# Cross attention normalised through the rows that shift its scores, with a new order on every engine

## The chip, the cores and the metric

The kernel runs on one core of a Trainium2 chip. A core has a matrix engine (TensorE, PE, whose weight loads the profile lists apart as PEld), a vector engine (VectorE, DVE), a scalar engine (ScalarE, ACT), a general engine (GpSimd, POOL) and DMA queues, which SyncE (SP), ACT and POOL feed. Each engine works through its own instructions strictly in order and waits on semaphores. The metric is the device time of one execution in microseconds.

## What is computed

Eight batches of 512 tokens by 512 features pass through two layers, each behind a layer norm and each added to its input.

```python
# cross attention: 16 heads of 32, 77 context tokens, masked by length
q, k, v = heads(ln(x) @ Wq), heads(ctx @ Wk), heads(ctx @ Wv)
A = softmax(where(mask, q @ k.T / sqrt(32), -1e20))       # 512 x 77 per head
x = x + (A @ v) @ Wo
# self attention: q, k, v and o are each a main matrix plus two low-rank experts,
# which a small gate picks for the whole batch element
h = ln(x); top, gates = top2(relu(mean(h) @ gw1.T) @ gw2.T)
x = x + o(softmax(q(h) @ k(h).T * SCALE) @ v(h))          # 512 x 512 per head
```

## The kernel before

All matrix work is on PE, batch after batch. In each layer 16 heads are four jobs of four heads. Cross attention of batch b, job i, goes like this. `q1` projects the normalised x; its result is split in a high and a low part and copied by ACT (`q1_rows`) and DMAs into a stack of rows, so that one product over 96 rows is exact enough. `csc` computes, for each of the four token tiles t, the scores of the four heads side by side in one PSUM bank (128 tokens by 4 x 78), and DVE takes the negated row maxima from it (L1040). `cross_shift` turns the 16 columns of maxima into 16 rows on PE (L1280), DVE splits these in high and low part (L1055, L1057), and ACT issues two small DMAs (`move_shift`, L900) that put the two parts into the stack as two further rows. `csT` (L1295) then computes the scores transposed, keys by tokens, and the two extra rows subtract each token's maximum in the same product. ACT takes exp (L914) into `probs1`. `cpv` (L1311) multiplies these with V, and `cden` (L1319) multiplies the same probabilities with ones, which gives the row sums, spread over the head's 32 rows. ACT copies the product of `cpv` out (`cacc`, L930, into the tile that the profile calls xhat), DVE takes the reciprocal of the sums in four pieces (`cinv`, L1075), POOL multiplies (`cdivide`, L754), and `out1` (L1217 with Wo) projects. Four jobs are summed in `out1`, so its last quarter needs job 3. Then come DVE's `residual1`, the second layer norm, the transposes (`xpose`, L1211), the gate, the effective weights (`weff`), and self attention with the same pattern: `sc` (L1274, row maxima at L1048), `shift`, `sT` (L1302, exp at L925), `pv` (L1331), sums over keys on POOL (`psum`, L780 and L784), `den` (L1340), `inv` (L1075), `divide` (L754), `out2` (L1217).

Scores of both layers share a ring of two PSUM banks, transposed scores another of two, and three banks (`pj`) go to whatever step needs one. The cross attention of batch b+1 is interleaved with the self attention of batch b, so the pattern repeats with every batch. Only batch 0's cross attention has no self attention beside it. There PE also runs the products of the context (`context_keys`, L1190; `context_values`, L1202) and dummy products (`warm`, L1182).

What sets the order is a table: `CALENDAR` gives a time to each step of a batch, `OWN` gives exceptions, and every engine walks through all steps in the order of these times and issues its part of each (`Engine.walk`). The times are no clock: they only sort. Semaphore waits are computed from the same order.

## Time and profile before

| | |
|---|---|
| three runs | 1421.96, 1423.52, 1429.27 us (median 1423.52) |
| span of the profiled execution | 1426.7 us, from the first to the last instruction |
| PE busy | 1391.0 us, 97% |
| DVE, ACT, POOL busy | 951.9 us (67%), 861.3 us (60%), 679.8 us (48%) |
| mean granted TensorE clock | 0.980 of full |
| PE's share of the chain that ended last | 85% |

No time is given for the profiled execution apart from its span, and the span is 3.2 us above the median of the runs. A busy share is an average. The chain that ended last is followed back from the last instruction: each piece of it is what the next one had to wait for. A clock of 1.00 in a stretch is 2.4 GHz, and 0.50 is 1.2 GHz.

### The profile page before, as it was taken

How to read it: one execution, taken by the hardware profiler on the slowest of the kernel's cores; microseconds unless marked ns; L12 is line 12 of the kernel's file. 1: busy time of each engine (PE TensorE's matmuls, PEld its weight loads, DVE VectorE, ACT ScalarE, POOL GpSimd, SP SyncE). 2: the span in 40 equal slices, each digit the busy share in tenths (PEclk: the TensorE clock that was granted, in tenths of full speed). 3: DMA queues.
4: the chain of work that ended last, by engine and by line, in shares of the span. 5: the costliest groups of instructions: out<-in, count | busy, mean ns of one | idle time of the engine just before them, and what ended most of it. 6: DMA issues, size and time to landing. Idle time of an engine off the chain costs nothing.

```text
span 1426.7 us, 17122 instructions
## 1 busy us (share of the span) xinstructions
PE 1391.0 (97%) x5704; PEld 702.4 (49%) x5704; DVE 951.9 (67%) x1687; ACT 861.3 (60%) x1499; POOL 679.8 (48%) x411
## 2 busy tenths in 40 slices
PE   8998999999999999999999999999999999999987
PEld 5545444545455444555555445455545454444432
DVE  4454577766767677767777677767777677666572
ACT  2425474866577663975658664876648665565652
POOL 2011143545555362556445463555625455465675
PEclk9889999999999999999999999999999999999999
DMA  7514233522434224522234224332235323233210
GB/s 252 143 53 133 46 68 96 153 76 46 98 110 108 75 54 125 137 61 76 68 111 123 75 59 135 110 85 67 58 104 152 76 46 97 64 101 79 81 39 30
DMA packets 78767, 130.81 MB, mean 92 GB/s; under 512 B 26374, under 2 KB 32134, under 8 KB 75607
## 3 DMA queue, kind: packets, MB, share of 16 engines
q1 hardware_dynamic: 74007, 128.55, 33.4%
q10 hardware_dynamic: 4672, 1.17, 0.4%
q8 instruction: 45, 0.74, 0.2%
q14 instruction: 43, 0.35, 0.1%
HBM read 66.08 MB, written 12.21 MB: 55 GB/s over the span
## 4 chain that ended last, share of the span: by engine, by line
PE 85%; ACT 7%; issue 2%; DMA 2%; POOL 2%; DVE 1%; ACTq 0%; SPq 0%; POOLq 0%
PE pj L1217 43%; PE scT L1302 9%; PE sc L1274 8%; PE acc L1331 7%; PE sc L1263 4%; PE pj L1247 2%; PE pj L1311 2%; PE scT L1295 2%; PE pj L1319 2%; PE pj L1340 2%; DMA qs<-shift 2%; PE pj L1190 1%; ACT xhat L810 1%; PE pj L1202 1%; PE pj L1211 1%
## 5 line engine op out<-in xcount | busy, mean ns | idle before, releaser
L925 ACT ACTIVATE probs<-scT 128x512 f32<-128x512 f32 x512 | 288.9, 594 | 303.9 <-PE scT L1302 300.8
L1048 DVE TENSOR_REDUCE negmax<-sc 128x1 f32<-128x512 f32 x512 | 338.0, 684 | 140.7 <-PE sc L1274 139.7
L784 POOL TENSOR_TENSOR probs_sum<-probs_sum,probs 128x1024 f32<-128x1024 f32 x128 | 300.2, 2365 | 57.4 <-ACT probs L925 57.3
L1075 DVE RECIPROCAL inv_sum<-pj 128x128 f32<-128x128 f32 x256 | 225.0, 921 | 59.9 <-PE pj L1340 39.2
L1274 PE MATMUL sc<-ks,qs 96*128 96x512 f32 x512 | 260.1, 541 | 2.4 <-DVE negmax L1048 1.6
L1217 PE MATMUL pj<-XT,Wqk 128*128 128x512 f32 x512 | 257.3, 598 | 0.6 <-DVE Wqk L1140 0.6
L1302 PE MATMUL scT<-qs,ks 99*128 99x512 f32 x512 | 250.9, 517 | 6.2 <-DMA qs<-shift 3.2
L780 POOL TENSOR_TENSOR probs_sum<-probs 128x1024 f32<-128x1024 f32 x64 | 151.4, 2372 | 173.8 <-ACT probs L925 173.8
L790 POOL TENSOR_TENSOR uv_stack<-UVS_sb,uv_stack 96x1024 fp32r<-96x1024 f32 x32 | 75.7, 2367 | 178.1 <-ACT UVS_sb L832 178.1
L1302 PEld LDWEIGHTS scT<-qs,ks 99*128 99x128 f32 x512 | 94.7, 191 | 124.5 <-ACT probs L925 60.4
L754 POOL TENSOR_TENSOR xhat<-xhat,inv_sum 128x128 f32<-128x128 f32 (+1 forms) x56 | 45.1, 806 | 207.7 <-DVE inv_sum L1075 207.7
L1274 PEld LDWEIGHTS sc<-ks,qs 96*128 96x128 f32 x512 | 97.9, 192 | 92.0 <-issue 47.1
L1331 PE MATMUL acc<-probs,V 128*32 128x512 f32 x1024 | 137.2, 613 | 0.0
L1217 PE MATMUL pj<-Wvo,ctx2T 128*128 128x512 f32 x256 | 131.0, 602 | 0.7 <-POOL ctx2T L754 0.7
L1217 PE MATMUL pj<-XT,Wq_sb 128*128 128x512 f32 x256 | 127.2, 601 | 1.1 <-ACT XT L844 1.1
L914 ACT ACTIVATE probs<-scT 77x512 f32<-77x512 f32 x128 | 72.4, 588 | 91.2 <-PE scT L1295 91.0
L1217 PE MATMUL pj<-Wvo,XT 128*128 128x512 f32 x256 | 122.4, 600 | 0.0
L1217 PEld LDWEIGHTS pj<-XT,Wqk 128*128 128x128 f32 x512 | 95.2, 191 | 54.7 <-issue 35.4
L1217 PE MATMUL pj<-Wo_sb,xhat 128*128 128x512 f32 x256 | 115.8, 599 | 0.0
L1263 PEld LDWEIGHTS sc<-keys,qsc 97*128 97x128 f32 x480 | 66.1, 196 | 34.5 <-issue 23.5
L893 ACT ACTIVATE ks<-stage_hi 32x512 fp32r<-32x512 f32 x128 | 80.1, 626 | 3.3 <-ACT stage_hi L868 0.6
L893 ACT ACTIVATE qs<-stage_hi 32x512 fp32r<-32x512 f32 x128 | 80.2, 626 | 2.7
(103 smaller groups left out, 1716.6 us busy)
## 6 DMA issues: line engine op xcount, KB each, us to landing
Wqk<-in_WmT SPq DMA_DIRECT2D x16, 1024.0 KB, 6.1
Wvo<-in_WmT SPq DMA_DIRECT2D x16, 1024.0 KB, 6.5
UVS_sb<-in_UVS SPq DMA_DIRECT2D x64, 192.8 KB, 3.4
qs<-stage_lo SPq DMA_DIRECT2D x136, 64.0 KB, 2.2
qs<-qs SPq DMA_DIRECT2D x34, 256.0 KB, 3.0
X<-in_x SPq DMA_DIRECT2D x8, 1024.0 KB, 6.0
ks<-stage_lo SPq DMA_DIRECT2D x128, 64.0 KB, 2.0
ks<-ks SPq DMA_DIRECT2D x32, 256.0 KB, 3.0
```

The costliest lines, as they stand in the source:

```text
L780: nc.gpsimd.tensor_tensor(probs_sum[:, pair], probs[:, 0, pair], probs[:, 1, pair], ALU.add)\
L784: nc.gpsimd.tensor_tensor(probs_sum[:, pair], probs_sum[:, pair], probs[:, kt % 2, pair], ALU.add)\
L790: nc.gpsimd.tensor_tensor(uv_stack[:].rearrange("p s n -> p (s n)"), UVS_sb[:, n, 0:2 * D], uv_stack[:].rearrange("p s n -> p (s n)").bitc ...
L893: nc.scalar.activation(stack[0:DH, slot, jj, :], stage_hi[jj * DH:(jj + 1) * DH, n, :].bitcast(F32), ACT.Copy).then_inc(sems["rows_copied" ...
L925: nc.scalar.activation(probs[:, kt % 2, jj, :], scT[:, ST[step], :], ACT.Exp, scale=SCALE)\
L1048: nc.vector.tensor_reduce(negmax[:, 0, n:n + 1], sc[:, SC[step], :], AX.X, ALU.max, negate=True)\
L1075: nc.vector.reciprocal(inv_sum[:, INV[use], at], pj[:, PJ[left_in(full)], at])\
L1217: mm = nc.tensor.matmul(pj[:, p, :], lhsT, rhs, start=(dc == 0), stop=(dc == DC - 1))
L1263: mm = nc.tensor.matmul(sc[:, SC[step], j * NKP:(j + 1) * NKP], cross_stack(b, i)[0:MASK_ROW + 1, j, t * P:(t + 1) * P], keys1[0:MASK_ROW ...
L1274: nc.tensor.matmul(sc[:, SC[step], :], qs[0:3 * DH, slot, jj, t * P:(t + 1) * P], ks[0:3 * DH, slot, jj, :], start=True, stop=True).then_i ...
L1302: nc.tensor.matmul(scT[:, ST[step], :], ks[0:ROWS, slot, jj, kt * P:(kt + 1) * P], qs[0:ROWS, slot, jj, :], start=True, stop=True).then_in ...
L1331: mm = nc.tensor.matmul(acc[jj * DH:(jj + 1) * DH, 0, :], V2[:, kt, v_slot(b, j), jj * DH:(jj + 1) * DH], probs[:, kt % 2, jj, :], start=( ...
```

## The change

Row sums are no longer found on PE from the finished probabilities, but on DVE and ACT from the untransposed scores, before the transposed product. For each tile t of `csc`, DVE adds the negated maximum to the scores (`cless`, 128 x 312, from PSUM to SBUF), ACT takes exp in place (`cexp`), and DVE sums each head's 77 columns (`csum`). For each job ACT takes the logarithm of the 16 sums per token (`cln`), and DVE scales it by -1/SCALE beside the maxima. `cross_shift` turns 32 columns instead of 16, ACT issues four small DMAs instead of two, and the stack gets two more rows. `csT` subtracts maximum and logarithm together, and exp gives probabilities that are divided already. `cden`, `cinv` and `cdivide` are gone; `out1` waits only for `cacc`. `csc`'s bank is released by `cless` instead of by the row maxima. The buffer of reciprocals shrinks to one, so `inv` of a job waits for `divide` of the job before. A table set that holds both exp and log is named at ACT's start. The layer norm of the next batch waits for `gate_top` of this batch.

```diff
-    "cden": (-963, -556, -444, -35),
+    "cln": (-1339, -1033.2, -557.9, -171),
...
+CROSS_ROWS = SHIFT_ROW + 4
+INVERSES = 1
+LESS_SLOTS = 2
...
     if kind == "cross_shift_move":
-        return {"cross_shift_moved": 32}
+        return {"cross_shift_moved": 64}
...
-INV, INV_BEFORE = ring([step for step in STEPS if step[0] in ("divide", "cdivide") and step[3] == pieces(step[2]) - 1], 2)
+INV, INV_BEFORE = ring([step for step in STEPS if step[0] == "divide" and step[3] == pieces(step[2]) - 1], INVERSES)
+LESS, LESS_BEFORE = ring([step for step in STEPS if step[0] == "cless"], LESS_SLOTS)
...
+            nc.scalar.preload_act_table_set("natural_log_exp_and_others")
...
             def normalize(step, b, half):
-                before = ("out1", b, TT - 1, DC - 1) if half else ("xpose", b - 1, 1, TT - 1)
+                before = ("out1", b, TT - 1, DC - 1) if half else ("gate_top", b - 1)
...
             def cross_shift_move(step, b, i):
-                move_shift(1, cross_stack(b, i), "cross_shift_moved", b, ("cross_shift", b, i))
+                dst = cross_stack(b, i)
+                for part, split in enumerate(("shift_hi", "shift_lo")):
+                    act.wait_ge(split, act.after(split, "cross_shift", b, i))
+                    for side in range(2):
+                        row, at = SHIFT_ROW + 2 * side + part, SIDE + side * HJ * TT
+                        queue.dma_start(dst[row:row + 1].rearrange("p j (t n) -> p (j t) n", n=P).bitcast(F32),
+                                        shift[at:at + HJ * TT, part, :].bitcast(F32)).then_inc(sems["cross_shift_moved"], 16)
...
+            def cexp(step, b, i, t):
+                act.wait_ge("cross_lessened", act.after("cross_lessened", "cless", b, i, t))
+                at = lessened[:, LESS["cless", b, i, t]]
+                nc.scalar.activation(at, at, ACT.Exp, scale=SCALE).then_inc(sems["cross_exped"], 1)
...
+                nc.scalar.activation(cross_sums[:], cross_sums[:], ACT.Ln).then_inc(sems["cross_ln"], 1)
...
+                nc.vector.tensor_tensor(lessened[:, LESS[step]],
+                                        sc[:, SC[scores], 0:HJ * NKP].rearrange("p (j k) -> p j k", j=HJ),
+                                        negmax[:, 1, t:HJ * TT:TT].rearrange("p (j a) -> p j a", a=1).to_broadcast([P, HJ, NKP]),
+                                        ALU.add).then_inc(sems["cross_lessened"], 1)
...
+                nc.vector.tensor_reduce(cross_sums[:, t:HJ * TT:TT], lessened[:, LESS["cless", b, i, t], :, 0:NK],
+                                        AX.X, ALU.add).then_inc(sems["cross_summed"], 1)
...
+                nc.vector.tensor_scalar(negmax[:, 1, HJ * TT:2 * HJ * TT], cross_sums[:], -1.0 / SCALE, None, ALU.mult)\
+                    .then_inc(sems["cross_scaled"], 1)
...
             def out1(step, b, t, dc):
                 pe.wait_ge("weights_loaded", 16 * 9)
-                pe.wait_ge("normed", pe.after("normed", "cdivide", b, dc, t * pieces(dc) // TT))
+                pe.wait_ge("pj_left_by_act", pe.after("pj_left_by_act", "cacc", b, dc))
...
-                nc.tensor.matmul(scT[0:NK, ST[step], :], keys1[0:ROWS, i, j, 0:NK], cross_stack(b, i)[0:ROWS, j, :],
+                nc.tensor.matmul(scT[0:NK, ST[step], :], keys1[0:CROSS_ROWS, i, j, 0:NK], cross_stack(b, i)[0:CROSS_ROWS, j, :],
...
-            def cden(step, b, i):
-                p = opened(left_in(step))
-                pe.wait_ge("exp_done", pe.after("exp_done", "csT", b, i, HJ - 1))
-                for j in range(HJ):
-                    mm = nc.tensor.matmul(pj[j * DH:(j + 1) * DH, p, :], ones[0:NK, :], probs1[0:NK, j, :],
```

Both tables are written anew, in every row. The order is shown at three places. In the listings an L number is a line of the version that it belongs to: after the change `q1` and `out1` stand at L1312, `context_keys` at L1285, `context_values` at L1297, `warm` at L1277, `csc` at L1358, `sc` at L1369, `cross_shift` at L1375 and `sT` at L1397; "x3" is three instructions alike.

The first place is PE in batch 0, up to the first `csc`, which reads `keys1`. Before, after the first twelve `q1`:

```order
L1190 MATMUL pj<-probs,Wqk 128x308 [waits pj_left_by_dve]
L1190 MATMUL pj<-probs,Wqk 128x308 x3
L1190 MATMUL pj<-probs,Wqk 128x308 [waits pj_left_by_dve]
L1190 MATMUL pj<-probs,Wqk 128x308 x3
L1217 MATMUL pj<-XT,Wq1_sb 128x512 [waits pj_left_by_dve]
L1263 MATMUL sc<-keys1,qsc 128x78 [waits q1_stacked0,keys1_loaded,consts_made]
L1263 MATMUL sc<-keys1,qsc 128x78 x7
L1217 MATMUL pj<-XT,Wq1_sb 128x512
L1263 MATMUL sc<-keys1,qsc 128x78 [waits rowmax_done]
L1263 MATMUL sc<-keys1,qsc 128x78 x3
L1263 MATMUL sc<-keys1,qsc 128x78 [waits rowmax_done]
L1263 MATMUL sc<-keys1,qsc 128x78 x3
```

After the change, from the last `q1` of the batch on:

```order
L1312 MATMUL pj<-XT,Wq1_sb 128x512
L1277 MATMUL acc<-Wq1_sb,ident_sb 128x128 x4
L1312 MATMUL pj<-XT,Wq1_sb 128x512 x4
L1277 MATMUL acc<-Wq1_sb,ident_sb 128x128 x3
L1285 MATMUL pj<-probs,Wqk 128x308 [waits pj_left_by_dve]
L1285 MATMUL pj<-probs,Wqk 128x308 x3
L1285 MATMUL pj<-probs,Wqk 128x308 [waits pj_left_by_dve]
L1285 MATMUL pj<-probs,Wqk 128x308 x3
L1285 MATMUL pj<-probs,Wqk 128x308 [waits pj_left_by_dve]
L1285 MATMUL pj<-probs,Wqk 128x308 x3
L1358 MATMUL sc<-keys1,qsc 128x78 [waits q1_stacked0,keys1_loaded,consts_made]
L1358 MATMUL sc<-keys1,qsc 128x78 x7
```

Before, 13 of the 16 `q1` and two groups of `context_keys` (L1190) stand between the transposes and the first `csc`; now all 16 `q1`, one group of `context_values` and three groups of `context_keys` do.

The second place is ACT in batch 0, around the shift of job 1. Before, from the exps of job 0 on:

```order
L914 ACTIVATE probs1<-scT 77x512 [waits scoresT_full] x2
L861 ACTIVATE stage_hi<-pj 128x512 [waits pj_full,q1_stacked0]
L914 ACTIVATE probs1<-scT 77x512 [waits scoresT_full] x2
L879 ACTIVATE qsc<-stage_hi 32x512 [waits stage_hi]
L879 ACTIVATE qsc<-stage_hi 32x512 x3
L900 DMA qs<-shift 1x16x128 [waits shift_hi]
L900 DMA qs<-shift 1x16x128 [waits shift_lo]
L837 ACTIVATE V2<-X 128x4x312 [waits pj_left_by_dve]
L914 ACTIVATE probs1<-scT 77x512 [waits scoresT_full,pj_full]
L914 ACTIVATE probs1<-scT 77x512 [waits scoresT_full] x3
```

After the change, from the shift of job 1 to the exps of its transposed scores:

```order
L982 ACTIVATE cross_sums<-cross_sums 128x16 [waits cross_summed,cross_scaled]
L989 ACTIVATE probs1<-scT 77x512 [waits scoresT_full] x2
L970 DMA qs<-shift 1x16x128 [waits shift_hi]
L970 DMA qs<-shift 1x16x128
L970 DMA qs<-shift 1x16x128 [waits shift_lo]
L970 DMA qs<-shift 1x16x128
L939 ACTIVATE qsc<-stage_hi 32x512 [waits stage_hi]
L939 ACTIVATE qsc<-stage_hi 32x512 x3
L976 ACTIVATE lessened<-lessened 128x312 [waits cross_lessened] x2
L897 ACTIVATE V2<-X 128x4x312 [waits pj_left_by_dve]
L989 ACTIVATE probs1<-scT 77x512 [waits scoresT_full,pj_full]
L989 ACTIVATE probs1<-scT 77x512 [waits scoresT_full]
```

Before, a shift is two issues and the next cross exps follow; now it is four issues, followed by four copies for the stack of another job, two `cexp` (L976) and the copy of V2.

The third place is PE in the steady part, batch 2 of the cross attention, job 1. Before, from `csc`'s first two tiles to its `cross_shift` (L1280):

```order
L1263 MATMUL sc<-keys1,qsc 128x78 x7
L1217 MATMUL pj<-Wvo,XT 128x512
L1263 MATMUL sc<-keys1,qsc 128x78 [waits rowmax_done]
L1263 MATMUL sc<-keys1,qsc 128x78 x3
L1302 MATMUL scT<-qs,ks 128x512
L1302 MATMUL scT<-qs,ks 128x512 [waits exp_done]
L1263 MATMUL sc<-keys1,qsc 128x78 [waits rowmax_done]
L1263 MATMUL sc<-keys1,qsc 128x78 x3
L1217 MATMUL pj<-XT,Wqk 128x512 [waits pj_left_by_dve]
L1274 MATMUL sc<-ks,qs 128x512 [waits rowmax_done,k_stacked0,q_stacked0]
L1302 MATMUL scT<-qs,ks 128x512 [waits exp_done]
L1280 MATMUL pj<-ident_sb,negmax 128x128 [waits rowmax_done,inverted]
```

After the change:

```order
L1312 MATMUL pj<-Wvo,XT 128x512 [waits inverted]
L1358 MATMUL sc<-keys1,qsc 128x78 [waits cross_lessened]
L1358 MATMUL sc<-keys1,qsc 128x78 x3
L1358 MATMUL sc<-keys1,qsc 128x78 [waits cross_lessened]
L1358 MATMUL sc<-keys1,qsc 128x78 x3
L1312 MATMUL pj<-Wvo,XT 128x512 x3
L1397 MATMUL scT<-qs,ks 128x512 [waits exp_done] x2
L1369 MATMUL sc<-ks,qs 128x512 [waits cross_lessened,k_stacked0,q_stacked0]
L1369 MATMUL sc<-ks,qs 128x512 [waits cross_lessened]
L1312 MATMUL pj<-XT,Wqk 128x512 [waits pj_left_by_dve]
L1312 MATMUL pj<-XT,Wqk 128x512
L1375 MATMUL pj<-ident_sb,negmax 128x128 [waits cross_scaled,pj_left_by_dve]
```

Each `csc` tile from the third on waited for row maxima, and now waits for `cless` (`cross_lessened`), as the next `sc` does; between the last tile and `cross_shift` stand five products into `pj` banks, two `sT` and two `sc`, where it was one of each, and `cross_shift` waits for the scaled logarithm (`cross_scaled`).

## Rows read from the trace of the kernel before

**Rows 1.** The page: busy us by engine, share of the span.
```profile
PE 1391.0 (97%) x5704; PEld 702.4 (49%) x5704; DVE 951.9 (67%) x1687; ACT 861.3 (60%) x1499; POOL 679.8 (48%) x411
```

**Rows 2.** The chain that ended last, by line.
```profile
by line: PE pj L1217 42.8%; PE scT L1302 8.7%; PE sc L1274 7.5%; PE acc L1331 7.2%; PE sc L1263 3.8%; issue 2.4%; PE pj L1247 2.3%; PE pj L1311 2.2%; PE scT L1295 2.2%; PE pj L1319 2.1%; PE pj L1340 1.6%; DMA qs<-shift 1.6%; PE pj L1190 1.3
```

**Rows 3.** Stretches: PE, PEld, DVE, ACT, POOL busy us, clock, DMA share, GB/s.
```profile
60.00:80.00 20.00, 19.23 (x82) 12.53 (x79) 11.05 (x18) 6.13 (x11) 1.27 (x1) 0.50 0.45 138
600.00:800.00 200.00, 199.07 (x841) 100.94 (x840) 141.38 (x252) 135.61 (x238) 104.07 (x59) 1.00 0.35 91
```

**Rows 4.** Chain that ended last, two windows: start us, us, what.
```profile
580.40 1.08 ACT probs L925 x2
...
744.21 1.08 ACT probs L925 x2
```

**Rows 5.** Waits of PE: line, releaser: us in total, times, longest us.
```profile
PE pj L1211 <- ACT XT L844: 4.0, 6, 0.7
PE pj L1280 <- DVE negmax L1048: 3.3, 4, 1.9
...
PE sc L1274 <- DVE negmax L1048: 1.6, 3, 0.7
```

**Rows 6.** Groups by form: shape, count | busy us, mean ns | idle before.
```profile
L1319 PE MATMUL pj<-probs,ones 77*32 77x512 f32 x256 | 35.5, 627 | 0.8 <-ACT probs L914 0.8
...
L1075 DVE RECIPROCAL inv_sum<-pj 128x128 f32<-128x128 f32 x256 | 225.0, 921 | 59.9 <-PE pj L1340 39.2 <-PE pj L1319 18.3 <-POOL ctx2T L754 1.9
L1040 DVE TENSOR_REDUCE negmax<-sc 128x4 f32<-128x312 f32 x128 | 59.3, 477 | 30.3 <-PE sc L1263 29.8
...
L985 DVE TENSOR_TENSOR X<-pj,X 128x308 f32<-128x308 f32 x8 | 3.8, 478 | 9.3 <-PE pj L1190 9.3
...
L914 ACT ACTIVATE probs<-scT 77x512 f32<-77x512 f32 x128 | 72.4, 588 | 91.2 <-PE scT L1295 91.0
...
L945 ACT ACTIVATE g<-top 128x1 f32<-128x1 f32 x8 | 2.3, 294 | 0.2
...
L810 ACT ACT_TABLE_LOAD x1 | 1.3, 1283 | 2.8 <-issue 2.8
```

**Rows 7.** Timeline, PE, batch 0: start us, us, line, operation, [idle before].
```profile
69.39 1.93 PE L1319 MATMUL pj<-probs,ones 77*32 77x512 f32 x8 [0.77 <-ACT probs L914]
...
87.72 1.04 PE L1319 MATMUL pj<-probs,ones 77*32 77x512 f32 x8
88.69 12.28 PE L1217 MATMUL pj<-Wo_sb,xhat 128*128 128x512 f32 x28
```

**Rows 8.** Timeline, PE, batch 0 up to its last cross transpose.
```profile
9.83 12.32 PE L1190 MATMUL pj<-probs,Wqk 128*128 128x308 f32 x40 [2.04 <-DMA Wqk<-in_Wk]
...
30.34 10.54 PE L1217 MATMUL pj<-XT,Wq_sb 128*128 128x512 f32 x24 [0.90 <-ACT XT L844]
40.72 4.31 PE L1190 MATMUL pj<-probs,Wqk 128*128 128x308 f32 x16
...
45.33 1.39 PE L1263 MATMUL sc<-keys,qsc 97*128 97x78 f32 x8
...
49.23 0.27 PE L1280 MATMUL pj<-ident_sb,negmax 128*128 128x128 f32 x1
...
77.31 0.41 PE L1280 MATMUL pj<-ident_sb,negmax 128*128 128x128 f32 x1
```

**Rows 9.** ACT's queue at one point; DMA group: KB, us to landing.
```profile
592.20 1.44 ACTq L900 DMA_DIRECT2D qs<-shift  x2
...
qsc<-shift ACTq DMA_DIRECT2D x60, 8.0 KB, 1.9
```

**Rows 10.** Timeline of the end.
```profile
1406.75 4.66 POOL L784 TENSOR_TENSOR probs_sum<-probs_sum,probs 128x1024 f32<-128x1024 f32 x2
...
1411.56 1.07 PE L1340 MATMUL pj<-probs_sum,ones 128*32 128x512 f32 x8 [1.73 <-POOL probs_sum L784]
...
1412.55 10.92 PE L1217 MATMUL pj<-Wvo,ctx2T 128*128 128x512 f32 x24
```

More of the change, by code:

```diff
@@ L255 @@
+    "divide": {(7, 0, 0): 19647, (7, 1, 0): 21807.3, (7, 2, 0): 21951.9, (7, 3, 0): 31067.8, (7, 3, 1): 31068.1,
[10 rows of a table added]
 }
@@ L349, in increments @@
     if kind == "cross_shift_move":
-        return {"cross_shift_moved": 32}
+        return {"cross_shift_moved": 64}
     if kind in ("csT", "sT"):
         return {"scoresT_full": 1, "exp_done": 1}
-    if kind in ("cpv", "cden", "den"):
+    if kind in ("cpv", "den"):
         return {"pj_full": 1}
+    if kind == "cless":
+        return {"cross_lessened": 1}
+    if kind == "cexp":
+        return {"cross_exped": 1}
+    if kind == "csum":
+        return {"cross_summed": 1}
+    if kind == "cln":
+        return {"cross_ln": 1, "cross_scaled": 1}
     if kind == "cacc":
         return {"pj_left_by_act": 1}
-    if kind in ("cinv", "inv"):
+    if kind == "inv":
         return {"inverted": 1}
-    if kind in ("cdivide", "divide"):
+    if kind == "divide":
         return {"normed": 1}
@@ L421 @@
 LEAVES = {"q1": ("q1_split", 2), "out1": ("residual1", 2), "qk": ("qk_split", 3), "v": ("v_bias", 2),
-          "out2": ("residual2", 2), "cpv": ("cacc", 2), "cden": ("cinv", 2), "den": ("inv", 2)}
-LAST_PART = ("cinv", "inv")
+          "out2": ("residual2", 2), "cpv": ("cacc", 2), "den": ("inv", 2)}
+LAST_PART = ("inv",)
 ITSELF = ("context_keys", "context_values", "xpose", "weff", "shift", "cross_shift", "gate_hidden", "gate_top")
@@ L434, in opens @@
 def opens(step):
-    return step[0] in ITSELF or step[0] in ("cpv", "cden", "den") or (step[0] in LEAVES and step[-1] == 0)
+    return step[0] in ITSELF or step[0] in ("cpv", "den") or (step[0] in LEAVES and step[-1] == 0)
 def banks(size):
@@ L1073, in inverse @@
                     dve.wait_ge("normed", dve.after("normed", *INV_BEFORE[use]))
-                dve.wait_ge("pj_full", dve.after("pj_full", *full))
-                nc.vector.reciprocal(inv_sum[:, INV[use], at], pj[:, PJ[left_in(full)], at])\
+                dve.wait_ge("pj_full", dve.after("pj_full", "den", b, j))
+                nc.vector.reciprocal(inv_sum[:, INV[use], at], pj[:, PJ[left_in(("den", b, j))], at])\
                     .then_inc(sems["inverted"], 1)
-            def cinv(step, b, i, part):
-                inverse(("cden", b, i), ("cdivide", b, i, pieces(i) - 1), part)
-            def inv(step, b, j, part):
-                inverse(("den", b, j), ("divide", b, j, pieces(j) - 1), part)
             def residual1(step, b, t):
```

325 lines of the change are left out of this document (179 added, 146 removed), and 223 rows, old and new, of tables (CALENDAR, OWN).

## Prediction

> **What bounds the kernel now.** I read the busy times first: PE works 1391.0 of 1426.7 us, DVE 67%, ACT 60%, POOL 48% [rows 1]. That is an average, so next the chain that ended last by line: its long entries are PE lines, and `cden` (L1319) is 2.1% of it, 30.0 us, so its products stand on the path and not beside it [rows 2]. Then the stretches: from 600 to 800 us PE is busy 199.07 of 200 us at full clock, while ACT has 135.61 and DVE 141.38 [rows 3]. The same exp of the chain comes at 580.40 and at 744.21 us, so a batch takes 163.8 us [rows 4], of which PE works 163. PE's waits are small: the largest sum on one line is 4.0 us in the whole run, and the row maxima of `sc` hold it up for 1.6 us [rows 5]. So in the steady part the time is PE's work, and what leaves PE leaves the time, if no new wait replaces it.
>
> Two stretches differ. From 60 to 80 us, batch 0's cross jobs, PE looks busy for 19.23 us but at a clock of 0.50, that is 1.2 GHz, with dummy products among its work [rows 3]. There the chain from maxima through shift to exp decides. And the last `den` waits 1.73 us for POOL's sums, then 24 products end the kernel [rows 10].
>
> **`cden` goes.** 30.0 us on the chain over 32 steps are 0.94 us each [rows 2]; one in sight, from 87.72 to the next start at 88.69, took 0.97 [rows 7]. The four of batch 0 lie in the stretch that PE does not bound (the one at 69.39 lasts 1.93 at half clock [rows 7]), and I count them in the start below. The other 28 give 28 x 0.94 = **-26.3 us**.
>
> **`cinv` and `cdivide` go.** 128 reciprocals of 0.92 us leave DVE, 14.7 us per batch [rows 6]. In steady batches they stood beside PE's work, so nothing comes off directly. They pay for what is added: per batch 16 `cless` (nearest row L985, 128x308 from PSUM, 0.48) and 16 `csum` (nearest L1040, 128x312 reduced, 0.48) are 15.3 us, and 4 scalings under 0.3 each [rows 6]. DVE's load stays about level, at 70%.
>
> **ACT gets more.** Per batch 16 `cexp` between 0.29 (128x1) and 0.59 (77x512), taken at 0.48 because 312 columns lie nearer to the latter; 4 `Ln` of 16 columns at 0.3 [rows 6]; 8 more issues at 0.5 to 0.72 us, since ACT stands while it issues (two took 1.44 [rows 9]). That is 7.7 + 1.2 + 4 to 5.8 = 13 to 15 us on top of 111 (135.61 x 163.8/200), 125 of some 160. ACT stays under PE, but each piece sits in a queue in strict order, ahead of exps that PE waits for.
>
> **New waits in the steady part.** `csc`'s bank is now held through the maxima and `cless`, 0.96 us instead of 0.48 [rows 6]. The order answers this: between the second and third tile stand four products (the listing shows the last of them), and between the last tile and `cross_shift` nine where there were three. From the last tile to the shifted rows the new chain is `cless` 0.48, `cexp` 0.48, `csum` 0.48, `Ln` 0.3, scaling 0.2 = 1.9 us, plus four hand-overs of 0.15 (POOL's sum ends at 1411.41, `den` starts at 1411.56 [rows 10]) = 2.5 us. Five of the nine are projections of 0.88 us each (twelve took 10.54 [rows 8]), 4.4 us, so on time it is covered; late by a busy ACT it is not. Behind PE's wait stand `sc` and `sT`; behind DVE's wait for `cexp` stand the row maxima. Between 0 and 12 us in all, since old waits on such lines came to a few us each [rows 5]; I take 0.6 per batch over seven, **+4 us**. The single buffer of reciprocals lies in these too: `inv` waits for `divide` of the job before, which has most of a quarter batch (41 us) for it.
>
> **The start.** Before, `q1` begins at 30.34 and the first `csc` at 45.33 [rows 8]. In the new order one group of `context_keys` (2.2 us, half of 4.31) and one of `context_values` (eight products at 0.44, 3.5 us) no longer stand ahead of the transposes, so `q1` may begin near 25. But then come all 16 `q1` (0.88 each, 14.1 us), that `context_values` (3.5) and three groups of `context_keys` (6.5), with a few dummies: 25 us, so the first `csc` is at 50 to 51, **5 later**. Each cross job had 9.4 us from one transposition of maxima to the next (49.23 to 77.31 over three [rows 8]). The longer chain fits into that except for job 2, where ACT first issues four DMAs (2.6), makes four copies and V2 ahead of or among its `cexp`: about **2 more**. The last job has its 2.5 us of chain uncovered, since nothing but dummies can fill PE. That is 9.5, less some work moved forward. `out1`, which ended at 100.97 (88.69 + 12.28 [rows 7]), would end near 110: **+9 us**, between +3 (PE takes up the moved `q1` and the four missing `cden`, 6 us together) and +15 (each job adds its 2 us).
>
> The granted clock speaks against the start as well: 0.50 in the 20 us in which PE waits for such chains [rows 3]. The Trainium skill (TensorE: Matmul & The Clock Gate, Part 1) says that the throttled state is the default and that activity releases it. By that rule, taking products out of this stretch can lengthen it; the row agrees as far as it goes, and ten more microseconds at 0.50 would do five of work, an estimate of +5 to the sum below. I leave it in the range, since the moved `q1` and `context_keys` run densely ahead of the jobs.
>
> **The end.** The sums on POOL that the last `den` waits for remain. After it 10 instead of 12 `out2` stand, each two of the 24 products in 10.92 us [rows 10]: **-1.8 us**.
>
> **Sum.** 1426.7 - 26.3 + 9 + 4 - 1.8 = 1411.6 us of the span. The median of the runs lay 3.2 us under that span, so 1408.4, **1409 us**.
>
> **Rivals.** *Full gain:* the start absorbs its longer chain because the 3 `q1` moved forward no longer stand in it, and no new wait comes: start +4 to the sum with 30.0 for all `cden`, 1426.7 - 30.0 + 4 - 1.8 - 3.2 = 1396 us. For it speaks that ACT and DVE have a fifth of their time free; against it the strict chain at half clock. *Gain eaten:* start +15 and 1.7 us of waits in each of seven batches: 1426.7 - 26.3 + 15 + 12 - 1.8 - 3.2 = 1422 us. *Slower:* the score bank is the place. DVE, in order, stands at `csum` for an ACT that is issuing DMAs or copying, and so does not take maxima or do the next `cless`; PE finds both banks held. If half of the 128 `csc` tiles cost PE the longer hold of 0.53 us (0.48 and part of a hand-over), that is +34 in place of +4: 1439 us. It decides from some 19 us of such waits on, 0.15 us per tile. Against it speak the products that the order has put between tiles, and the small waits on row maxima so far [rows 5]. *The change doesn't do what it says:* `Ln` and exp would alternate between table sets, two loads for each of 32 `Ln`. The only load before took 1.283 us [rows 6]; 64 of them are 82 us of ACT, at worst all exposed: near 1487 us. The Trainium skill (ScalarE: Activation LUTs, Table sets: the hidden batching unit) lists one set that has both functions, so that no switch is needed; no run so far has a `Ln`. The changed program holds a single table load on ACT.
>
> **How the numbers follow.** Forecast 0.50 (1402 to 1416), full gain 0.19, gain eaten 0.18, slower 0.12, table loads 0.01. The time is the forecast's. The range runs from the full gain less the bounds on the waits to the gain eaten with its bound, 1393 to 1426, and leaves out most of the slower case and the ends. A measurement of this kernel can tell about 0.5% from no change, 1416.4 and 1430.6 us. Faster by more: the forecast nearly whole, full gain, little of the eaten: 0.67. Within: 0.20. Slower: 0.13.
>
> **What would show it.** Right: no L1319 in the chain, a batch of about 160.6 us in steady state (163.8 - 3.76 + 0.6), PE still busy 99% there, ACT near 155 of 200 us, the first `csc` near 50, `out1` of batch 0 ending near 110, and 20 products after the last `den`. The steady term is wrong if PE shows waits on `cless`, on the scaled logarithm or on exps of more than 2 us per batch. The start is wrong if `out1` ends before 104 or after 116. The whole is wrong if the batch period does not fall under 163.

## The result

The change made the kernel slower: 1452.88 us (median of 1447.59 to 1456.39) against 1422.74 us before, a ratio of 1.0202 [1.0174, 1.0231]. The forecast was 1409 us and its range ended at 1426; the chance of slower was given as 0.13. The profiled execution took 1450.59 us, its span is 1448.0 us, and the forecast in span terms was 1411.6.

The busy times of after, on its page, answer to [rows 1]:

```profile
PE 1387.6 (96%) x5448; PEld 697.5 (48%) x5448; DVE 981.3 (68%) x1847; ACT 905.1 (63%) x1659; POOL 635.4 (44%) x355
```

PE has 256 instructions less, the `cden`, which took 30 us of the chain, yet it is busy for only 3.4 us less: the others took longer, a first sign of the clock. Next come the stages of both kernels as stretches of the span: up to the moment when PE begins the gate (`gate_hidden`) of batch 0, to that of batch 1, to that of batch 7, and the rest. The columns are those of [rows 3]. Before:

```profile
0.00:113.00 113.00, 105.73 (x396) 61.28 (x397) 59.02 (x109) 36.86 (x59) 15.41 (x22) 0.88 0.49 149
113.00:251.50 138.50, 132.27 (x515) 67.41 (x516) 83.84 (x155) 77.67 (x135) 42.12 (x28) 0.96 0.32 83
251.50:1235.80 984.30, 978.20 (x4141) 494.85 (x4140) 696.13 (x1243) 641.97 (x1123) 504.33 (x301) 1.00 0.34 90
1235.80:1426.70 190.90, 174.79 (x654) 78.85 (x653) 112.95 (x184) 104.76 (x184) 117.98 (x62) 0.95 0.26 72
```

After:

```profile
0.00:123.20 123.20, 102.20 (x350) 58.44 (x351) 59.25 (x132) 43.91 (x79) 11.01 (x17) 0.88 0.46 143
123.20:266.90 143.70, 133.89 (x498) 68.51 (x498) 87.65 (x177) 85.13 (x156) 36.32 (x21) 0.94 0.32 82
266.90:1257.40 990.50, 977.32 (x3949) 492.62 (x3950) 722.46 (x1357) 672.64 (x1242) 470.39 (x258) 0.99 0.34 90
1257.40:1448.00 190.60, 174.22 (x654) 77.95 (x652) 111.94 (x184) 103.43 (x184) 117.67 (x61) 0.96 0.25 67
```

The third stretch is six steady batches. The forecast had it fall by 19.1 us (26.3 less 4 over seven batches is 3.19 a batch, and this stretch has six); it rose by 6.2. PE has 192 products fewer there and is busy just as long, at a clock of 0.99 where it was 1.00. The table sets the stages beside the forecast and beside the experiments told below (us; a column is the length of that stage in the profiled execution):

| kernel | to gate 0 | gate 0 to 1 | six steady batches | rest | span |
|---|---|---|---|---|---|
| before | 113.0 | 138.5 | 984.3 | 190.9 | 1426.7 |
| forecast | 122.0 | 135.3 | 965.2 | 189.1 | 1411.6 |
| after | 123.2 | 143.7 | 990.5 | 190.6 | 1448.0 |
| scaling on ACT | 123.2 | 144.4 | 970.1 | 189.1 | 1426.8 |
| the same, batch 0 by the old method | 109.4 | 142.2 | 971.3 | 191.0 | 1413.9 |

So after missed the forecast by 1.2 us in the start, 8.4 in the second stage, 25.3 in the steady part and 1.5 at the end, 36.4 in all. Each row is one execution, and the start alone moves from one to another: the row "batch 0 by the old method" runs the same 396 products in the same order up to gate 0 as before, in 109.4 us where before has 113.0.

Where it went shows in the waits of PE in after (they answer to [rows 5]):

```profile
PE pj L1375 <- DVE negmax L1167: 6.6, 9, 1.0
PE sc L1358 <- DVE lessened L1151: 5.8, 8, 1.9
PE pj L1342 <- DVE stage_lo L1106: 4.1, 6, 0.7
```

The line that leads, L1167, is `cln`'s scaling on DVE: 128 x 16 numbers times -1/SCALE, from SBUF to SBUF. The groups by form give the new operations' prices (they answer to [rows 6]):

```profile
L1151 DVE TENSOR_TENSOR lessened<-sc,negmax 128x312 f32<-128x312 f32 x128 | 60.6, 479 | 9.6
L1160 DVE TENSOR_REDUCE cross_sums<-lessened 128x4 f32<-128x308 f32 x128 | 57.7, 467 | 17.8 <-ACT lessened L976 14.3
L1167 DVE TENSOR_SCALAR negmax<-cross_sums 128x16 f32<-128x16 f32 x32 | 23.4, 731 | 14.0 <-ACT cross_sums L982 14.0
...
L976 ACT ACTIVATE lessened<-lessened 128x312 f32<-128x312 f32 x128 | 57.4, 461 | 72.7 <-DVE lessened L1151 72.2
L982 ACT ACTIVATE cross_sums<-cross_sums 128x16 f32<-128x16 f32 x32 | 6.9, 216 | 13.5 <-DVE cross_sums L1160 13.3
```

`cless`, `csum` and `cexp` cost what the prediction said (0.479, 0.467 and 0.461 us for 0.48 each), `Ln` less (0.216 for 0.3). The scaling has a mean of 731 ns where "under 0.3" stood, and a mean hides most of it. All instances of the line, shortest, median and longest:

```profile
L1167 DVE TENSOR_SCALAR negmax<-cross_sums x32: 174/176/2471, 56.9 to 1219.7; 128x16 f32<-128x16 f32 x32
```

The median is 176 ns, and the longest takes fourteen times as much. One of the long ones, on DVE's timeline (start, us, what):

```profile
635.69 0.84 DVE L1160 TENSOR_REDUCE cross_sums<-lessened 128x4 f32<-128x308 f32 x2
636.88 2.33 DVE L1167 TENSOR_SCALAR negmax<-cross_sums 128x16 f32<-128x16 f32 x1 [0.34 <-ACT cross_sums L982]
639.13 0.68 DVE L1123 TENSOR_REDUCE negmax<-sc 128x1 f32<-128x512 f32 x1
```

and what POOL did at that time:

```profile
635.51 2.36 POOL L850 TENSOR_TENSOR uv_stack<-UVS_sb,uv_stack 96x1024 fp32r<-96x1024 f32 x1 [5.17 <-ACT UVS_sb L892]
637.84 1.26 POOL L822 TENSOR_TENSOR ctx2T<-ctx2T,inv_sum 128x512 f32<-128x512 f32 x1
639.07 7.01 POOL L844 TENSOR_TENSOR probs_sum<-probs_sum,probs 128x1024 f32<-128x1024 f32 x3
```

The scaling began while L850 ran on POOL, stood through the rest of it and through the next, and ended at 639.21, where L822 ended (639.10) and not before. Over all 32: the 18 that met no POOL instruction took 174 to 177 ns, and the 14 that met one took 704 to 2471 ns and ended within 0.12 us after the end of one, eight of them the first, six the second in a row. What PE made of this one, on its timeline:

```profile
637.91 0.50 PE L1397 MATMUL scT<-qs,ks 99*128 99x512 f32 x1
639.27 0.33 PE L1375 MATMUL pj<-ident_sb,negmax 128*128 128x128 f32 x1 [0.85 <-DVE negmax L1167]
639.35 0.47 PE L1342 MATMUL pj<-uv_stack 96*128 96x512 f32 x1
640.52 0.51 PE L1342 MATMUL pj<-uv_stack 96*128 96x512 f32 x1 [0.69 <-DVE stage_lo L1106]
```

Between the end of `sT` and `cross_shift` (L1375) PE stood, and then again for `stage_lo`, which had been queued on DVE behind the scaling. Behind these two gaps the clock falls. Eight microseconds of after, from 39.85 us behind a gate on, and then the same stretch behind the same gate in e1, the kernel with the scaling on ACT told below:

```profile
638.00:646.00 8.00, 6.45 (x16) 3.74 (x17) 6.29 (x11) 3.25 (x6) 8.00 (x4) 0.79 0.15 37
```

```profile
630.50:638.50 8.00, 8.00 (x25) 4.25 (x25) 6.00 (x11) 5.01 (x9) 8.00 (x4) 1.00 0.15 37
```

Between the gates of batches 1 and 7, after has 23.9 us at 0.50 in all; before and the kernel with the scaling on ACT have none there. At half clock 23.9 us do at most 12.0 us of work less. The steady part of after is 20.4 us longer than with the scaling on ACT, which would leave 8.4 for the standing itself. But one of the six batches, from 762.94 to 926.63, had both waits and no fall of the clock: 163.69 us, 2.2 more than a batch with the scaling on ACT, while the five others took 164.4 to 166.4. Six times 2.2 are 13, which would leave 7 for the clock. So the clock makes between 7 and 12 of the 20.4, and these traces do not say it closer.

### The profile page after: what moved, and what is told of

Same layout as the page of the kernel before. It is cut to its first block, busy times and chain, and to the rows that moved or that the text cites. A ratio compares the mean times of both kernels' runs of the same rounds, so it can differ in the third digit from the quotient of the medians.

```text
span 1448.0 us, 17119 instructions
## 1 busy us (share of the span) xinstructions
PE 1387.6 (96%) x5448; PEld 697.5 (48%) x5448; DVE 981.3 (68%) x1847; ACT 905.1 (63%) x1659; POOL 635.4 (44%) x355
## 4 chain that ended last, share of the span: by engine, by line
PE 74%; DVE 12%; ACT 7%; issue 3%; POOL 2%; DMA 1%; ACTq 1%; SPq 0%; DVEq 0%; POOLq 0%
PE pj L1312 39%; PE scT L1397 7%; PE acc L1418 6%; PE sc L1369 6%; PE sc L1358 2%; DVE negmax L1123 2%; PE pj L1427 2%; PE scT L1390 2%; PE pj L1406 2%; PE pj L1342 2%; DVE negmax L1167 1%; PE pj L1297 1%; ACT probs L1000 1%; ACT ks L953 1%; ACT xhat L870 1%
## 5 line engine op out<-in xcount | busy, mean ns | idle before, releaser
L1000 ACT ACTIVATE probs<-scT 128x512 f32<-128x512 f32 x512 | 279.4, 593 | 198.3 <-PE scT L1397 162.1
L844 POOL TENSOR_TENSOR probs_sum<-probs_sum,probs 128x1024 f32<-128x1024 f32 x128 | 298.9, 2365 | 31.7 <-ACT probs L1000 31.6
L1312 PE MATMUL pj<-XT,Wqk 128*128 128x512 f32 x512 | 251.4, 598 | 1.1 <-DVE stage_lo L1099 1.0
L1369 PE MATMUL sc<-ks,qs 96*128 96x512 f32 x512 | 239.0, 519 | 6.2 <-DVE negmax L1123 2.4
L1397 PE MATMUL scT<-qs,ks 99*128 99x512 f32 x512 | 211.8, 482 | 5.7 <-ACT probs L1000 3.7
L850 POOL TENSOR_TENSOR uv_stack<-UVS_sb,uv_stack 96x1024 fp32r<-96x1024 f32 x32 | 75.7, 2366 | 208.5 <-ACT UVS_sb L892 208.5
L1397 PEld LDWEIGHTS scT<-qs,ks 99*128 99x128 f32 x512 | 92.5, 193 | 119.7 <-issue 60.0
L812 POOL TENSOR_TENSOR rstd<-vareps,minus_half 128x4 f32<-128x4 f32 x16 | 16.3, 1019 | 298.3 <-DVE minus_mean L1094 298.3
L1369 PEld LDWEIGHTS sc<-ks,qs 96*128 96x128 f32 x512 | 97.5, 193 | 95.0 <-DVE negmax L1123 41.7
L1176 DVE RECIPROCAL inv_sum<-pj 128x128 f32<-128x128 f32 x128 | 109.7, 913 | 31.1 <-PE pj L1427 30.9
L1312 PE MATMUL pj<-Wvo,XT 128*128 128x512 f32 x256 | 127.0, 626 | 0.2 <-DVE Wvo L1235 0.2
L1312 PE MATMUL pj<-Wvo,ctx2T 128*128 128x512 f32 x256 | 123.0, 605 | 3.0 <-POOL ctx2T L822 3.0
L1312 PEld LDWEIGHTS pj<-XT,Wqk 128*128 128x128 f32 x512 | 95.2, 191 | 61.9 <-issue 44.4
L1312 PE MATMUL pj<-XT,Wq_sb 128*128 128x512 f32 x256 | 122.7, 598 | 2.0 <-ACT XT L904 2.0
L1312 PE MATMUL pj<-Wo_sb,xhat 128*128 128x512 f32 x256 | 121.1, 609 | 0.1
L976 ACT ACTIVATE lessened<-lessened 128x312 f32<-128x312 f32 x128 | 57.4, 461 | 72.7 <-DVE lessened L1151 72.2
L822 POOL TENSOR_TENSOR ctx2T<-ctx2T,inv_sum 128x128 f32<-128x128 f32 (+1 forms) x56 | 45.0, 804 | 108.6 <-DVE inv_sum L1176 69.7
```

Of the source, the lines that this page charges most:

```text
L844: nc.gpsimd.tensor_tensor(probs_sum[:, pair], probs_sum[:, pair], probs[:, kt % 2, pair], ALU.add)\
L850: nc.gpsimd.tensor_tensor(uv_stack[:].rearrange("p s n -> p (s n)"), UVS_sb[:, n, 0:2 * D], uv_stack[:].rearrange("p s n -> p (s n)").bitc ...
L1000: nc.scalar.activation(probs[:, kt % 2, jj, :], scT[:, ST[step], :], ACT.Exp, scale=SCALE)\
L1176: nc.vector.reciprocal(inv_sum[:, INV[use], at], pj[:, PJ[left_in(("den", b, j))], at])\
L1312: mm = nc.tensor.matmul(pj[:, p, :], lhsT, rhs, start=(dc == 0), stop=(dc == DC - 1))
L1369: nc.tensor.matmul(sc[:, SC[step], :], qs[0:3 * DH, slot, jj, t * P:(t + 1) * P], ks[0:3 * DH, slot, jj, :], start=True, stop=True).then_i ...
```

## Experiments

**Is it the scaling?** The first theory is the one above. Its rivals were that the new order, the score bank held through `cless`, or other new waits cost the time. The scaling moved to ACT, right behind `Ln`, on the same order (e1):

```diff
+                nc.scalar.activation(negmax[:, 1, HJ * TT:2 * HJ * TT], cross_sums[:], ACT.Copy, scale=-1.0 / SCALE)\
+                    .then_inc(sems["cross_scaled"], 1)
...
-                nc.vector.tensor_scalar(negmax[:, 1, HJ * TT:2 * HJ * TT], cross_sums[:], -1.0 / SCALE, None, ALU.mult)\
-                    .then_inc(sems["cross_scaled"], 1)
```

> The changed kernel with one step moved: the scaling of the logarithms (L1167, 128x16 from SBUF to SBUF) is done by ACT right behind the Ln instead of by DVE. Theory A: in the changed kernel this DVE instruction takes 0.18 us where POOL is idle and 0.7 to 2.47 us where POOL is at work beside it, and the long ones (2.3 us, once per batch, POOL in three products back to back) hold up the row maxima, the transposition of the shift and weff behind them on DVE, so that PE stands still twice for about 1 us and then runs some us at 1.2 GHz. Then the batch period falls from 165.1 by 2 to 4 us and the whole time by 12 to 28 us, to about 1425 to 1440. Rival B: the bank of csc that is held through cless, and ACT's longer queue, are the cost: then the time stays within 5 us of 1452.9.

Measured: 1430.1 us, 1.0042 [1.0024, 1.0059] of before, 22.8 us under after. Its second stage and its steady part:

```profile
123.20:267.60 144.40, 135.56 (x497) 69.74 (x498) 85.99 (x173) 85.97 (x159) 36.25 (x21) 0.93 0.31 81
267.60:1237.70 970.10, 965.21 (x3948) 486.49 (x3949) 704.06 (x1332) 675.92 (x1266) 470.52 (x258) 1.00 0.35 92
```

Five of its six steady periods are from 161.48 to 161.52 and one is 162.58. The stall costs 20.4 of the 25.3 us by which the steady part had missed the forecast, and nothing in the second stage. Even without it the kernel lies above the forecast's range.

**Is it every DVE instruction of this kind?** `gate_hidden` also writes 128 x 128 numbers from SBUF to SBUF by `tensor_scalar`, once per batch, and in after it took 1.04 to 1.65 us in seven of eight cases, beside POOL's sums. In e2 ACT does it too:

```diff
+                nc.scalar.activation(hiddenB, ident_sb[:], ACT.Identity, bias=hidden[:, 0:1], scale=0.0)\
+                    .then_inc(sems["gate_step"], 1)
...
-                nc.vector.tensor_scalar(hiddenB, ident_sb[:], 0.0, hidden[:, 0:1], ALU.mult, ALU.add)\
-                    .then_inc(sems["gate_step"], 1)
```

> As the run before, and besides the gate's hidden vector is spread over 128 columns (L1202) by ACT instead of DVE. In the changed kernel it takes 1.04 to 1.65 us on DVE in seven batches where POOL sums probabilities beside it, against 0.28 us in the kernel before. Theory A: another 0.5 to 1.2 us per batch, 3 to 8 us in all on top of the first run. Rival: PE has other work there, and the gate's chain is not what PE waits for: under 2 us.

Measured: 1432.75 us, 1.0053 [1.0035, 1.0071]. No gain: this instruction stalls too, but PE waited for it once, 0.8 us, in all of after. What a stall costs is decided by who stands behind it.

There is a third instruction of this kind, which none of the runs moves. `vareps` in the layer norm is a `tensor_scalar` of 128 x 4, and all its instances in after are:

```profile
L1093 DVE TENSOR_SCALAR vareps<-meanvar x16: 169/170/2022, 15.3 to 1246.9; 128x4 f32<-128x4 f32 x16
```

Six of the 16 met POOL's `probs_sum` additions and took 1.72 to 2.02 us; the same six do so in the kernel with the scaling on ACT, and in before none does, 169 to 170 ns each. So the changed kernel has a second stall of some 2 us once per batch except at the ends of the run, and no run shows what it costs.

**Kind of instruction, or its place in the queue?** Both experiments start from e1, where ACT scales. e7 puts a spare `tensor_scalar` where the scaling was on DVE, and nothing reads its output; e8 puts a `tensor_reduce` of the same size there:

```diff
+                dve.wait_ge("cross_ln", dve.after("cross_ln", *step))
+                nc.vector.tensor_scalar(lessened[:, LESS["cless", b, i, TT - 1], 0, 0:HJ * TT], cross_sums[:], -1.0 / SCALE, None, ALU.mult)
```

```diff
+                dve.wait_ge("cross_ln", dve.after("cross_ln", *step))
+                nc.vector.tensor_reduce(lessened[:, LESS["cless", b, i, TT - 1], 0, 0:HJ * TT], cross_sums[:].rearrange("p (n a) -> p n a", a=1), AX.X, ALU.add)
```

> The first run's kernel (logarithms scaled on ACT), and on DVE, where the scaling stood in the changed kernel, a spare instruction of the same kind (tensor_scalar, 128x16, SBUF to SBUF) whose result nobody reads. Theory A1 (DVE's tensor_scalar from SBUF to SBUF cannot run while POOL works, and DVE's other instructions stand behind it): the spare instruction takes up to 2.3 us where POOL is busy, as L1167 did, and the time goes up by 10 to 22 us on the first run's 1430, although nothing waits for its result. Rival A2 (what cost was that PE and ACT waited for the scaled logarithm itself): within 4 us of 1430.

> The same as the run before, but the spare instruction is a tensor_reduce of the same 128x16 elements from SBUF to SBUF. Theory A1: it takes some 0.1 to 0.2 us whether POOL works or not, and the time stays within 4 us of the first run's 1430. Rival A3 (any DVE instruction at that place, waiting for Ln in DVE's order, does the harm): 1440 us or more.

Measured: e7 1446.4 us, 1.0154 [1.0108, 1.0199]; e8 1431.72 us, 1.0057 [1.0039, 1.0075], where e1 has 1.0042. All instances of the spare instruction, in e7 and then in e8:

```profile
L1169 DVE TENSOR_SCALAR lessened<-cross_sums x32: 174/176/2458, 57.3 to 1217.8; 128x16 f32<-128x16 f32 x32
```

```profile
L1169 DVE TENSOR_REDUCE lessened<-cross_sums x32: 169/170/171, 57.7 to 1202.9; 128x16 f32<-128x16 f32 x32
```

Same place, same size, same wait for `Ln`, and in each kernel 14 of the 32 ran while POOL worked: the one takes up to 2458 ns, the other never over 171. So it is the kind of instruction that meets POOL, not the queue or the wait for ACT. And an instruction that nobody waits for cost 15 us against e8, since DVE work that PE needs stands behind it in order: in each of the six steady batches of e7 PE waits 1.75 to 1.92 us for `stage_lo`. These batches took 984.7 us in e7 and 969.7 in e8. The Trainium skill ("SBUF — State Buffer", section "Who interferes with whom") says that VectorE and GpSimd share one pair of ports under an exclusive lock, so that the later of the two stands still until the other is done, and that `tensor_scalar` can take that pair while `tensor_reduce` on trn2 cannot. The two rows agree. They add that the loser can stand through two POOL instructions in a row, as six of the 14 long ones in after did.

**Method or order?** e3 is the new method on the old tables, with the new steps put right behind those that they need; e4 the old method on the new tables:

```diff
+                times["cless", b, i, t] = csc[t] + 0.3
+                times["cexp", b, i, t] = csc[t] + 0.4
...
+            times["cross_shift", b, i] = max(times["cross_shift", b, i], times["csc", b, i, 3] + SHIFT_AFTER)
```

> The changed kernel's way of dividing, in the order of the kernel before: the old tables, with cless, cexp, csum and cln put behind each csc, and the shift of a cross job at least 2.7 us behind its last scores. Theory O (the new order is at fault, the method gives what was forecast): 1400 to 1418 us, with a batch period near 161. Theory M (the method costs as much as cden gave, in any order): 1430 us or more. The DVE scaling is left on DVE, so where POOL is at work beside it some stalls remain.

```diff
+            times["cden", b, i] = done + 0.01 if i == 3 or (b, i) == (0, 2) else times["cpv", b, i] + 0.02
+            for part in range(FOUR_PARTS):
+                times["cinv", b, i, part] = times["cden", b, i] + 0.01 + 0.005 * part
```

> The kernel before's way of dividing (cden, cinv, cdivide), in the order of the changed kernel, these steps put right behind cpv or cacc. If the new order by itself is worse than the old: 1450 to 1490 us. If the order is as good and only the method costs: 1420 to 1435 us.

Measured: 1553.99 us, 1.0904 [1.0875, 1.0934], and 1549.43 us, 1.086 [1.0827, 1.0893]. The pair is inconclusive. Each method on the other's tables takes 9% longer than before, so the tables belong to their methods, and a part of the change cannot be priced by crossing them. PE's largest waits, in e3 for the scaling again and in e4 for the reciprocals, are about a quarter of each loss:

```profile
PE pj L1361 <- DVE negmax L1153: 35.1, 14, 4.4
```

```profile
PE pj L1284 <- DVE inv_sum L1142: 30.6, 18, 2.7
```

**What holds the rest: the score bank?** e5 is e1 without the cross attention's maxima: ACT takes exp straight from `csc`'s bank, DVE's `csc` maxima and `cless` are gone, and a shift is two DMAs again. It leaves out the subtraction of the maximum.

```diff
-                nc.scalar.activation(at, at, ACT.Exp, scale=SCALE).then_inc(sems["cross_exped"], 1)
+                nc.scalar.activation(lessened[:, LESS[step]], sc[:, SC[scores], 0:HJ * NKP].rearrange("p (j k) -> p j k", j=HJ),
+                                     ACT.Exp, scale=SCALE).then_inc(sems["cross_exped"], 1)
```

> The first run's kernel (logarithms scaled on ACT) without the maxima of the cross scores: no row maximum and no cless on DVE, ACT takes exp straight from csc's bank and frees it, the shift has one pair of rows again and two DMAs per job. The maximum that softmax may subtract is left out; the scores of this input are small enough for it. It takes 15 us per batch from DVE, and 4 DMA issues of 0.6 us per batch from ACT, and ends the hold of csc's bank through cless. Theory B (hold of the bank, DVE and ACT's issues make up what is left of the gap: batch 0 to the gate 10 us late, from there to the next gate 6 us longer than before instead of 3 us shorter, 0.8 us per steady batch): the start comes back by 3 to 6 us, the stretch from batch 0 to 1 by 3 to 6, the steady batch by 0.5 to 0.8, in all 9 to 17 us, to about 1413 to 1421. Rival: the order, tuned for other lengths, holds it: within 4 us of the first run.

Measured: 1423.08 us, 0.9996 [0.9981, 1.001], where e1 has 1.0042. In the profiled executions the start is 1.7 us shorter (121.5) and the next stage 3.2 (141.2), while the six steady batches stay, 969.6 against 970.1:

```profile
262.70:1232.30 969.60, 965.10 (x3949) 486.44 (x3950) 623.82 (x1141) 674.04 (x1266) 470.73 (x258) 1.00 0.35 92
```

Little of the 1.7 us can be told from chance: e2, whose PE runs the same products as e1's up to gate 0, came there at 122.0 where e1 has 123.2. So neither the longer hold of the bank, nor 13 us of DVE work per batch, nor two more issues cost anything in the steady part.

**The start.** Its forecast was nearly right, and two experiments ask what it hangs on. e6 is e1 with the last `q1` group of batch 0 moved behind the first `csc`; e9 is e5 (without maxima) with ACT's copies for job 3 and the copy of V2 moved behind job 2's exps:

```diff
+    for dc in FOUR:
+        times["q1", 0, 3, dc] = -593.9 + 0.1 * dc
```

> The first run's kernel with the last four q1 steps of batch 0 (job 3, 3.5 us on PE) put behind the last csc tile of job 0 instead of ahead of the first one. If the order ahead of the first csc is what makes it 5.4 us later than in the kernel before, the first csc comes near 47.3 instead of 50.7 and the gate of batch 0 about 2 to 3.5 us earlier than 123.2. Rival (the chain of the jobs on DVE and ACT, with the copies for job 3 in it, decides): the gate moves by less than 1 us, or later.

```diff
+    times["q1_rows", 0, 3] = -399.38
+    times["q1_stack", 0, 3] = -399.37
+    times["split_keys", 1] = -205.6
```

> The kernel without the maxima (1423.1 us), and in batch 0 ACT's four copies for job 3 and the copy of V2 stand behind the exps of job 2's scores instead of ahead of them. Theory (they hold up job 2 by some 3 us, PE waited 3.73 us for that exp): the gate of batch 0 comes 2 to 4 us earlier than 121.5, the whole 2 to 5 us, to 1418 to 1421. Rival (job 3's copies are needed as urgently, and the delay only moves): within 1 us.

Measured: e6, run once, 1430.44 us; its first `csc` comes at 47.13 instead of 50.74, yet gate 0 at 124.74 instead of 123.17. e9 1423.75 us, 0.9999 [0.9978, 1.002]; gate 0 at 122.71 where e5 has 121.49. Neither is a gain, and the losses, 1.6 and 1.2 us, are of the size of the 1.2 us between e1 and e2. In e6 the first `csc` came 3.6 us earlier and gate 0 did not follow, so that moment alone does not set the start. That the sequence of jobs on DVE and ACT does is argued, not shown.

**A version that beats both.** If the start's loss belongs to the new method and its order where PE has nothing else to do, batch 0 should keep the old one. e10 takes batch 0's cross attention with `cden`, `cinv`, `cdivide` and the old tables up to gate 0, and everything behind it as in e1. e11 leaves out the maxima from batch 1 on as well.

```diff
+    first = {step: time for step, time in old.items() if time < old["gate_hidden", 0]}
+    second = {step: time for step, time in new.items()
...
+    steps = sorted(first, key=first.get) + sorted(second, key=second.get)
```

> Batch 0's cross attention as in the kernel before (cden, cinv, cdivide, and the old order up to the gate of batch 0), all else as in the first run (logarithms scaled on ACT, the new order). Theory: the start is lost to the longer chain from scores to shift, and nothing after the gate of batch 0 depends on it: the gate comes at 113 us as before instead of 123.2, and the whole is 9 to 11 us shorter than the first run's 1430, near 1420. Rival: later stretches (batch 0 to 1) take up what the start gives, since transfers or the clock hold them: the whole is within 5 us of 1430.

> As the run before, and from batch 1 on without the maxima of the cross scores (left out as in the earlier run without them). Theory: gate of batch 0 at 113 us, the stretch to the next gate 141 us as in that run, steady batches 161.7, end 189: 1413 of span and 1414 to 1416 us, faster than the kernel before by about half a per cent. Rival: as above, about 1422.

Measured: e10 1415.01 us, 0.9939 [0.9919, 0.9959]; e11 1412.18 us, 0.9926 [0.9903, 0.9949]. The stages of e10:

```profile
0.00:109.40 109.40, 101.09 (x396) 58.66 (x396) 58.78 (x109) 36.94 (x59) 15.40 (x22) 0.92 0.50 154
109.40:251.60 142.20, 132.86 (x484) 67.54 (x484) 86.57 (x179) 86.03 (x160) 37.53 (x23) 0.94 0.34 87
251.60:1222.90 971.30, 966.47 (x3948) 487.24 (x3949) 704.13 (x1332) 676.54 (x1266) 470.37 (x258) 1.00 0.35 92
1222.90:1413.90 191.00, 175.44 (x654) 78.68 (x652) 111.97 (x184) 103.48 (x184) 117.75 (x61) 0.94 0.25 66
```

Gate 1 stands at 251.6 as in the kernel before: gate 0 comes 3.6 us earlier, and the second stage takes 3.7 longer although batch 1's 32 products of `cden` have left it (484 against 515 in the trace). Then the steady part is 13.0 us shorter, the whole gain in span. The medians gain less, 0.61% or 8.7 us, since the profiled execution of before is one of its longer ones. e11 is not told apart from e10 by these intervals.

## Why the prediction was wrong

**The step that failed: "4 scalings under 0.3 each".** It cost 22.8 of the 44 us between the forecast and the median, and it is not the only one: with the scaling on ACT the kernel is still 21 us over the forecast and above its range (about 9 in the second stage, 5 in the steady part, 1 in the start and 6 to 7 between span and median, all told below). Its place was the paragraph on DVE's load, where the scaling was priced by its size and by rows of other shapes, and then counted once more as 0.2 in the chain from `csc` to the shifted rows. Size was not what it costs. With POOL idle 0.176 us is even under the price; with POOL at work it is 0.70 to 2.47, 20.2 us on the 14 instances where 2.5 were due. Yet the trace of before held a row that says so, which is not among the rows of the prediction: `gate_hidden`'s `tensor_scalar`, all its instances:

```profile
L1107 DVE TENSOR_SCALAR hiddenB<-ident_sb,hidden x8: 277/279/1331, 114.4 to 1237.1; 128x128 f32<-128x128 f32 x8
```

Seven of eight took some 0.28 us, and the one of 1.33 us, at 1237.14, ran beside this:

```profile
1236.03 6.96 POOL L784 TENSOR_TENSOR probs_sum<-probs_sum,probs 128x1024 f32<-128x1024 f32 x3
```

With that row the scaling's bound would have been one POOL instruction, up to 2.4 us; that a stall can last through two, only the new kernel showed. The prediction also counted no time for what stands behind the scaling on DVE. Its own sign, waits of PE of more than 2 us per batch, would have missed the case: the two gaps come to 1.5 us per batch. The period, 165.1 where it had to fall under 163, gave it away.

**"New waits +4" (0 to 12).** With the scaling on ACT the steady period is 970.1 / 6 = 161.7 us. It fell by 2.4 us, where the removal less the waits was to give 3.2, so 1.4 of the 3.76 for `cden` did not come off instead of 0.6. That lies within the bound, but the word "waits" is not borne out: PE's idle time in the steady part is 6.1 us before and 4.9 in e1 (length less busy), while its busy time fell by 13.0 us, 2.2 per batch. What keeps the other products busy longer stays open. One new wait is there, 0.37 to 0.39 us per batch for the gate's input (`pooled`), which stands on DVE behind the stalled `vareps`; in before none is recorded there. In after itself the loss was far over the bound, and PE's waits in the profile tell only a part: 7 to 12 of the 20.4 us came as a lower clock after them. The prediction named the clock in the start alone. That a steady stage at 1.00 loses it after two gaps of about a microsecond or less had no term.

**The start, +9.** Near in size against the profiled execution of before: +10.2 in after and in e1. A part of that is luck. e10 and e11 run batch 0's products in the order of before and reached gate 0 at 109.4 and 105.5, with a granted clock of 0.92 and 0.97 where before's execution had 0.88; e11 (its 397th product is the gate's first):

```profile
0.00:105.50 105.50, 95.54 (x397) 56.24 (x397) 58.58 (x110) 36.93 (x59) 15.42 (x22) 0.97 0.53 160
```

Against these the new start costs 13.8 to 16.0 us (e1 against e10, e5 against e11). Two of its marks held: the first `csc` at 50.55 (predicted 50 to 51), and `out1` of batch 0 ending at 112.3 (predicted near 110, wrong only over 116):

```profile
50.55 1.21 PE L1358 MATMUL sc<-keys,qsc 97*128 97x78 f32 x8
...
102.62 9.71 PE L1312 MATMUL pj<-Wo_sb,xhat 128*128 128x512 f32 x22
112.17 7.03 PE L1297 MATMUL pj<-Wvo,probs 128*128 128x512 f32 x16
```

And job 2 is the long one, as said. From one `cross_shift` to the next it is 10.4, 12.7 and 9.7 us, where 9.4 was the mean before, and ACT's queue shows the four issues, the four copies and the copy of V2 around its first `cexp`:

```profile
70.11 2.45 ACTq L970 DMA_DIRECT2D qs<-shift  x4
72.61 2.59 ACT L939 ACTIVATE qsc<-stage_hi 32x512 fp32r<-32x512 f32 x4 [2.14 <-issue]
75.22 0.82 ACT L976 ACTIVATE lessened<-lessened 128x312 f32<-128x312 f32 x2
75.94 1.23 ACT L897 ACTIVATE V<-X 128x1248 fp32r<-128x1248 f32 x1
```

**What had no term: from gate 0 to gate 1.** I counted that stage as one steady batch (-3.2) and it came out at +5.2. There the stall is not the cause: with the scaling on ACT the stage is still 144.4. PE stands idle for 9.8 us there in after and 8.8 in e1, for 6.2 before (length less busy), and the granted clock is 0.94 and 0.93 for 0.96. 3.2 us of it hang on the maxima, which e5 gives back; the rest is not resolved. Start and second stage together are what the new method with its order costs at the head of the kernel: gate 1 comes 16.0 us later in e1 than in e10, and 16.4 later in e5 than in e11. The medians of these pairs differ by 10 to 15 us.

**The end, -1.8.** The 20 products behind the last `den` are there (8.97 us where 24 took 10.92 [rows 10]), but the last stage lies between 188.7 and 192.5 us over the kernels in which it has the same instructions, so that 1.8 is not told from 190.9 before. **The table loads**: `ACT_TABLE_LOAD` occurs once in after, 1.3 us, so that rival was rightly small. **ACT near 155 of 200 us** was too high: it has 143.96 from 600 to 800. Per steady batch its busy time rose from 107.0 to 112.1 us where 13 to 15 were put down; the 4 to 5.8 for issues are not counted as busy, `Ln` and exp are a little shorter than priced, and some 3 us stay unexplained.

**The rivals.** The slower case was on the list at 0.12, at 1439 us, with a price of 34 us for the score bank. Its outcome came, but its mechanism didn't: e5 takes the bank's longer hold away and the steady part keeps its length. **From span to median** I took off 3.2 us, and after's median lies 4.9 above its span, which is 8 us of the miss: the profiled execution of before was among its longer ones (elsewhere a span lies 1.8 to 2.8 us under the time of its own execution, 2.6 in after, and one run of before has 1429.27), so that a stage table against it flatters the new kernels by up to 6 us. The ratios do not depend on it.
